# A node table seeded with its residual: x copied into the table in the first layer's down part, rows scaled before they are added

## What is computed

```
def _layer(x, node_idx, edge_idx, norm_n2e, norm_e2n, W_n2e, W_e2n):
    h = x @ W_n2e
    e = relu(segment_sum(norm_n2e * h[node_idx], edge_idx))
    n = segment_sum(norm_e2n * (e @ W_e2n)[edge_idx], node_idx)
x1 = relu(_layer(x, ..., W0_n2e, W0_e2n))
x2 = _layer(x1, ..., W1_n2e, W1_e2n)
x = layernorm(x + x2)
```

## Time and profile before

| what | value |
|---|---|
| time, median of 3 runs | 6743.85 us (6737.83 to 6748.29) |
| span of the profiled execution | 6891.4 us |
| share of the span busy: PE, DVE, ACT, POOL | 62%, 69%, 48%, 58% |
| DMA, mean over the span | 237 GB/s, 1634 MB in 646,111 packets |
| hardware queue (SP), software queue (POOL) | 1234.83 MB, 394.18 MB |

### The profile page before, as it was taken

How to read it: one execution, slowest core, us unless ns; L and a number is a source line. 1 busy time by engine, 2 the same in 40 slices (tenths; PEclk the granted TensorE clock), 3 DMA queues, 4 the chain that set the end, 5 groups by cost and what they waited for, 6 DMA issues and landing times. The chain is left out here.

```text
span 6891.4 us, 79060 instructions
## 1 busy us (share of the span) xinstructions
PE 4257.5 (62%) x18989; PEld 3141.2 (46%) x18989; DVE 4783.1 (69%) x15487; ACT 3305.7 (48%) x7376; POOL 4010.9 (58%) x3167
## 2 busy tenths in 40 slices
PE   2568883038885788499866677988885677600000
PEld 1247773037774666377612223547774566500000
DVE  6635544645454877599599996866665999587666
ACT  0023331013332555288656665758885788633333
POOL 4757776757775788767155426611113666277776
PEclk9779996569998999799978778989998899855555
DMA  7845445864544999799688988989996677477665
GB/s 278 287 121 79 76 75 147 335 197 75 79 76 89 328 350 351 219 326 342 200 293 304 312 273 318 379 290 328 331 336 222 231 258 247 175 261 242 236 227 193
DMA packets 646111, 1634.06 MB, mean 237 GB/s; under 512 B 128454, under 2 KB 283878, under 8 KB 630290
## 3 DMA queue, kind: packets, MB, share of 16 engines
q1 hardware_dynamic: 459954, 1234.83, 51.9%
q0 software_dynamic: 185696, 394.18, 21.4%
HBM read 816.50 MB, written 813.62 MB: 237 GB/s over the span
## 5 line engine op out<-in xcount | busy, mean ns | idle before, releaser
L822 POOL DMA_INDIRECT NS<-e_tot,e_idx x392 | 648.6, 1655 | 298.1 <-ACT e_tot L1080 222.4
L2304 ACT ACTIVATE l_z<-l_a,l_nb,l_rs 128x256 f32<-128x256 f32 x1176 | 612.7, 605 | 411.3 <-DMA out_dram<-l_z,k_ids 248.1
L1691 POOL DMA_INDIRECT l_eg<-HBT,k_nsrc x392 | 461.8, 1178 | 391.2 <-DVEq L1916 151.3
L956 DVE TENSOR_SCALAR e_eq<-e_pk,z_skey 128x128 f32<-128x128 f32 x588 | 204.2, 348 | 637.1 <-DMA NS<-e_tot,e_idx 608.1
L2181 POOL DMA_INDIRECT out_dram<-l_z,k_ids x392 | 432.0, 1102 | 150.9 <-issue 115.1
L1734 PE MATMUL l_pb<-l_jx,k_ones 128*128 128x128 f32 x26 | 4.3, 304 | 788.3 <-DVE l_jx L1971 788.3
L1080 ACT ACTIVATE e_tot<-e_pa 128x520 f32<-128x520 f32 x196 | 118.6, 605 | 759.7 <-DMA NS<-e_tot,e_idx 748.6
L2226 PE MATMUL l_pm<-k_w_L3b,l_zt 128*128 128x258 f32 x1568 | 404.5, 417 | 126.8 <-ACT l_o L2274 121.8
L2475 DVE BATCH_NORM_STATS2 l_bs<-l_a 128x6 f32<-128x256 f32 x1176 | 467.2, 420 | 10.5 <-issue 3.5
L1223 POOL DMA_INDIRECT XH<-n_o,z_home x392 | 398.0, 1015 | 118.1 <-issue 113.1
L2342 ACT ACTIVATE l_a<-l_a,l_eshare 128x64 f32<-128x64 f32 (+1 forms) x1372 | 382.0, 371 | 124.4 <-DVE l_eshare L1953 67.6
(11 more groups left out here) (409 smaller groups left out, 13538.8 us busy)
## 6 DMA issues: line engine op xcount, KB each, us to landing
NS<-z_zero SPq DMA_DIRECT2D x200, 520.0 KB
HBT<-l_o SPq DMA_DIRECT2D x196, 528.0 KB
l_a<-HBT SPq DMA_DIRECT2D x196, 528.0 KB
GSUMS<-l_erun SPq DMA_DIRECT2D x72, 1056.0 KB
l_a<-XH SPq DMA_DIRECT2D x98, 528.0 KB
HA<-n_o SPq DMA_DIRECT2D x98, 528.0 KB
l_a<-HA SPq DMA_DIRECT2D x98, 528.0 KB
n_r<-NS SPq DMA_DIRECT2D x98, 520.0 KB
```

The source lines that it names most:

```text
L822: pool.indirect_dma_start(out=nodes, out_offset=bass.IndirectOffsetOnAxis(ap=idx[q % DEEP][:, k:k + 1], axis=0), in_=tot[q % 2][:, k, :], ...
L1691: pool.indirect_dma_start(out=self.g[b % self.ng][:, k, :], out_offset=None, in_=self.table, in_offset=bass.IndirectOffsetOnAxis(ap=self.i ...
L2304: last = act.activation(z[:, j, 0:D], a[:, j, 0:D], ACT.Identity, bias=self.nb[b][:, col:col + 1], scale=self.rs[b][:, col:col + 1])
```

## The change

In layer e0's down part SP copies x into NS1, HBM to HBM, 512 rows a DMA in rows of 4 KB, two such copies behind each of the 49 loads of z, and clears the 256 spare rows and 128 rows past the last node. The 100 clears of NS1 in e1's up part are gone. `inv`, the scale of each edge's gathered row, is kept for all 49 tiles in e1; ACT's copy of a pair's total becomes two instructions of 256 columns with that scale, since the count of edges of a gathered node is also the count of the node that its edge goes back to. NS1 has rows of 256 columns, not 260, and already holds x when the sums are added. Node stage n0 loads NS1 alone into `a`, and has neither counts nor the addition; it has eight buffers each of `a` and `o`.

```diff
+def copy_rows(eng, table, x, n, sem):
+    if n == TAILN:
+        eng.dma_start(table[TAIL0:N, :]..., x[TAIL0:N, :]...).then_inc(sem, 16)
+    else:
+        eng.dma_start(table[n * BLK:(n + 1) * BLK, :].rearrange("(p j) w -> p (j w)", j=J),
+                      x[n * BLK:(n + 1) * BLK, :].rearrange("(p j) w -> p (j w)", j=J)).then_inc(sem, 16)
+def clear_spare_rows(eng, table, zero, sem):
+    spare = NPAD - 2 * P
+    eng.dma_start(table[spare:NPAD, :].rearrange("(p j) w -> p j w", j=2), zero[:, 0:2, 0:D]).then_inc(sem, 16)
+    eng.dma_start(table[N:N + P, :], zero[:, 0, 0:D]).then_inc(sem, 16)
...
+    filled = NREAL + 2 if scaled else CLEARS
-        inv = [s.sb(f"inv{b}", [P, J]) for b in range(2)]
+        inv = s.sb("inv", [P, TR, J]) if scaled else None
-        tot = [s.sb(f"tot{b}", [P, 2, SW]) for b in range(2)]
+        tot = [s.sb(f"tot{b}", [P, 2, ow]) for b in range(2)]
...
-                        pe.matmul(pa[:, 1, 0:SW], e[:, 1, :], mt[:, 1, :], start=True, stop=True).then_inc(s_tot, 1)
+                        pe.matmul(pa[:, 1, 0:ow], e[:, 1, :], mt[:, 1, 0:ow], start=True, stop=True).then_inc(s_tot, 1)
...
-                        act.activation(tot[q % 2][:], pa[:, :, 0:SW], ACT.Copy).then_inc(s_cp, 1)
+                        if scaled:
+                            for k in range(2):
+                                c = column(q) + k
+                                last = act.activation(tot[q % 2][:, k, :], pa[:, k, 0:ow], ACT.Copy, scale=inv[:, c // J, c % J:c % J + 1])
+                        else:
+                            last = act.activation(tot[q % 2][:], pa[:, :, 0:ow], ACT.Copy)
+                        last.then_inc(s_cp, 1)
...
                     sp.dma_start(z[n % RR][:], sumv[:, J * t:J * (t + 1), :]).then_inc(s_z[n % RR], 16)
+                    if seeds:
+                        seeded, sem, x = seeds
+                        if n == 0:
+                            clear_spare_rows(sp, seeded, S["zero"], sem)
+                        for c in range(NREAL * n // TR, NREAL * (n + 1) // TR):
+                            copy_rows(sp, seeded, x, c, sem)
...
-    RA, RR, RO = 7, 4, 7
+    RA, RO = 8, 8
...
-                            sp.dma_start(a[t % RA][:], A["x"][t * BLK:(t + 1) * BLK, :]...).then_inc(s_in[t % RA], 16)
-                        sp.dma_start(r[t % RR][:], T["NS1"][t * BLK:(t + 1) * BLK, :]...).then_inc(s_rin[t % RR], 16)
+                            sp.dma_start(a[t % RA][:], T["NS1"][t * BLK:(t + 1) * BLK, :]...).then_inc(s_in[t % RA], 16)
...
-        "NS1": nc.dram_tensor("NS1", (NPAD, SW), F32).ap(),
+        "NS1": nc.dram_tensor("NS1", (NPAD, D), F32).ap(),
...
-                                      up=(T["NS0"], S["cleared0"], EARLY, CLEARS), early=early,
+                                      up=(T["NS0"], S["cleared0"], EARLY, CLEARS), early=early, seeds=(T["NS1"], S["cleared1"], A["x"]),
-                                  up=(T["NS1"], S["cleared1"], 0, CLEARS), homes=(S, V, T), gather=T["HOME"])
+                                  up=(T["NS1"], S["cleared1"], 0, 0), homes=(S, V, T), gather=T["HOME"])
```

More of the change, by code:

```diff
@@ L681, in store, with hyper_layer_phase @@
                      self.T["HOME"].rearrange("(n p j) o -> p n (j o)", p=P, j=J)).then_inc(self.s_ho, 16)
-def hyper_layer_phase(nc, S, tag, table, tw, sums, w1, w2, nodes, clear, up, scatter=None, listing=None, homes=None, gather=None, early=None):
+def hyper_layer_phase(nc, S, tag, table, tw, sums, w1, w2, nodes, clear, up, scatter=None, listing=None, homes=None, gather=None, early=None, seeds=None):
     RR = 3
@@ L692, in hyper_layer_phase @@
     scaled = tw > D
+    ow = nodes.shape[1]
+    filled = NREAL + 2 if scaled else CLEARS
     with Scope(nc, tag) as s:
@@ L817, in _ @@
                         if q == 1:
-                            pool.wait_ge(clear, 16 * CLEARS)
+                            pool.wait_ge(clear, 16 * filled)
                         else:
@@ L1013, in _ @@
                         e, mt = eq[q % DEEP], m[q % DEEP]
-                        pe.matmul(pa[:, 0, 0:SW], e[:, 0, :], mt[:, 0, :], start=True, stop=False)
-                        pe.matmul(pa[:, 0, 0:SW], e[:, 2, :], mt[:, 1, :], start=False, stop=True)
-                        pe.matmul(pa[:, 1, 0:SW], e[:, 1, :], mt[:, 1, :], start=True, stop=True).then_inc(s_tot, 1)
+                        pe.matmul(pa[:, 0, 0:ow], e[:, 0, :], mt[:, 0, 0:ow], start=True, stop=False)
+                        pe.matmul(pa[:, 0, 0:ow], e[:, 2, :], mt[:, 1, 0:ow], start=False, stop=True)
+                        pe.matmul(pa[:, 1, 0:ow], e[:, 1, :], mt[:, 1, 0:ow], start=True, stop=True).then_inc(s_tot, 1)
                     if tick == EVICT:
@@ L1142, in first_nodes_phase @@
     TN = NREAL
-    LD, ADD, VAR, NORM, TURN, ZT, PROD, EVICT, STORE = 0, 2, 3, 5, 6, 7, 8, 9, 10
-    RA, RR, RO = 7, 4, 7
+    LD, STAT, VAR, NORM, TURN, ZT, PROD, EVICT, STORE = 0, 2, 3, 5, 6, 7, 8, 9, 10
+    RA, RO = 8, 8
     with Scope(nc, tag) as s:
         a = [s.sb(f"a{b}", [P, J, D]) for b in range(RA)]
-        r = [s.sb(f"r{b}", [P, J, SW]) for b in range(RR)]
         o = [s.sb(f"o{b}", [P, J, XW]) for b in range(RO)]
-        inv = [s.sb(f"inv{b}", [P, J]) for b in range(2)]
         bs = [s.sb(f"bs{b}", [P, 2 * J, 6]) for b in range(2)]
@@ L1170, in first_nodes_phase @@
         s_os = [s.pool_sem(S, f"out_scattered{b}") for b in range(RO)]
-        count_lk = Links(s.sem("count_steps"))
         stat_lk = Links(s.sem("row_stats_ready"))
@@ L1306, in variance, with stats @@
                     dve.tensor_scalar(ve[b][:], mv[b][:, :, 1], EPS, None, ALU.add).then_inc(s_var, 1)
[L1308 to L1313, removed]
-                    count_lk.link(dve.reciprocal(iv[:], iv[:]))
-                    yield
-                    count_lk.settle(dve)
+                def stats(t):
                     dve.wait_ge(s_in[t % RA], 16 * (t // RA + 1))
                     for j in range(J):
-                        last = dve.scalar_tensor_tensor(at[:, j, :], rt[:, j, 0:D], iv[:, j:j + 1], at[:, j, :], ALU.mult, ALU.add)
-                        if j < J - 1:
-                            yield
-                    last.then_inc(s_u, 1)
-                    yield
-                    dve.wait_ge(s_u, t + 1)
-                    for j in range(J):
-                        stat_lk.link(dve.bn_stats(bs[t // 2 % 2][:, t % 2 * J + j, :], at[:, j, :]))
+                        stat_lk.link(dve.bn_stats(bs[t // 2 % 2][:, t % 2 * J + j, :], a[t % RA][:, j, :]))
                         yield
@@ L1338, in _ @@
                         parts.append(variance(*q))
-                    if tile(tick, ADD) is not None:
-                        parts.append(add(tick - ADD))
+                    if tile(tick, STAT) is not None:
+                        parts.append(stats(tick - STAT))
                     take_turns(parts)
```

16 lines of the change are left out of this document (6 added, 10 removed).

## The result

The changed kernel took 6852.85 us, median of four runs (6839.86 to 6863.19), against 6743.44 us before on the same chip: 1.0154 times as long, 95% interval 1.0137 to 1.0172, +109 us. The sign was forecast; the forecast time, 6794 us, was 59 us too low, and the result lies 3 us above the range, 6690 to 6850 us.

What follows compares the result with a forecast made beforehand. It took the down parts as bound by chains of landing, two POOL issues and transfer, and n0 by POOL. Terms -32 - 30 - 10 + 122 = +50 us on 6743.85 gave 6794 us, range 6690 to 6850.

Steps and rivals of the forecast that it cites:

- Term 1: e1's up part: without the clears of NS1, shorter gathers, fewer DVE waits and an earlier end, -32 us (-20 to -40).
- Term 4: e0's down part: copies take turns with scatter-adds at 0.33 us a packet, +2.9 us in 42 pairs, +122 us.
- rival (a): e0's down part: copies run at one-sided pace, 0.163 us a packet, costing 57 us; net -15, 6729 us; chance 0.25.
- Term 2: Node stage n0 without counts, addition and second load: faster scatters and an earlier start, -30 us (-10 to -42).
- Term 3: e1's down part: shorter rows speed the scatter-adds and ACT's split copy costs nothing, -10 us.
- rival (d): e1's down part: ACT's copy on the chain, +25 us, or PE loses clock; 6819 us; chance 0.05.
- (b): e0's down part: copies hide in idle head and gap of each pair, costing 17 us; net -55, 6689 us; chance 0.19.
- (c): e0's down part: all copy work passes on and z comes late, 222 us; net +150, 6894 us; chance 0.08.

Runs made afterwards that it cites:

- e0: Not a run: a layer of the kernel, in whose down part the change places the copies; its adds take 672.4 us before, 807.2 after.
- e12_before: The kernel before, unedited, profiled on the chip where it runs in 6742 us; 6746.14 us, a single run.
- the first experiments: e1_before, e2_copy4k, e3_copy1k and e4_sbuf_fill, on a chip where the kernel before takes about 6890 us.
- e2_copy4k: Changed kernel with its copies cut into packets of 4 KB; 6989.16 us, 1.0143 of the kernel before on the same chip.
- e1_before: The kernel before, unedited, run again for a profile; 6890.52 us, ratio 0.9998.
- e3_copy1k: Changed kernel with its copies cut into rows of 1 KB; 6973.11 us, 1.0115 of the kernel before on the same chip.
- e4_sbuf_fill: Changed kernel writing zeros from SBUF in place of x, in packets of 4 KB; 6987.44 us, 1.013 of the kernel before.
- e13_after: The changed kernel, unedited, profiled on the same chip as e12_before; 6852.24 us, 1.0165 of the kernel before.
- e14_copy_e1up: Changed kernel with all 98 copies in e1's up part, in the clears' place, on the chip of e12_before; 6701.74 us, 0.9944 of the kernel before.
- e9_gate_two: Changed kernel with both copies held by a semaphore wait to the head of a pair without z; 6850.5 us, 0.9964 of the kernel before.
- e10_gate_one: Changed kernel with one copy at each of 42 heads of pairs without z, 14 before the first pair, 42 in e1's up part; 6839.71 us, 0.9948.

## Why the prediction was right, and where it was wrong

**Term 1, the clears (-32 us): the step that failed.** The step charged the clears with waits and a late end that they did not make, and took a gain of 32 us from leaving them out. Measured +5 us (290.8 to 295.7), which is no gain; the untouched stretches differ by nearly as much. The working took three numbers for the price of the clears: 13 us of gathers above 1.00 us, 8 us of waits for DVE, 12 us of a late end. The last two weren't the clears'. With clears, on a chip as fast as that of the timing (e12_before), the waits for DVE are 0.3 us in place of the earlier trace rows's 8.5, and between the last gather and the joining of the runs there are 7.6 us, not the 21 of the earlier trace rows:

```profile
1362.16 0.99 POOL L792 DMA_INDIRECT e_g<-NS,z_src  x1 [0.30 <-issue]
...
1369.79 0.50 PEld L1005 LDWEIGHTS e_po<-e_run,k_join 128*128 128x128 f32 x2 [268.34 <-DVEq L888]
```

What they were is in DVE's waits in this stretch (engine, tile, line, what it waited for: us, times, longest). The profile that the prediction read has

```profile
DVE e_run L885 <- issue: 30.9, 19, 4.2
...
DVE e_run L885 <- remote: 17.4, 10, 3.5
```

the kernel before again, on the chip of the first experiments,

```profile
DVE e_run L885 <- remote: 27.9, 15, 4.9
DVE e_run L885 <- issue: 21.3, 20, 2.7
DVE e_g L870 <- remote: 15.1, 10, 2.2
```

and on the chip of 6742 us, the same kernel and stretch:

```profile
DVE e_inv L863 <- DMA e_g<-NS,z_src: 85.1, 45, 6.3
```

On the chip of the first experiments, DVE stands between two steps of its own for 64 us, and no transfer ends those waits; on the last it hardly does (0.5 us). Taking the clears away there won 9 us in e2_copy4k (from the first gather to the joined rows 299.6 us, 308.9 in e1_before), 5 in e3_copy1k and 2 in e4_sbuf_fill. I had noted that the profile's span was 2.2% above the timing and carried a difference in us over from it; but most of this term was made of what sets the two chips apart. The 13 us of longer gathers were real in the row and not the clears' either: their mean is 1.049 us with clears and 1.071 without. What sets it is open.

**Term 4, the copies (+122 us): the size nearly right, by a wrong way.** Measured +134.8 us. In the two profiles of the changed kernel pairs with copies last 10.2 and 10.3 us and the others 6.8, as forecast; by 42 pairs the copies cost 3.2 us each (134.8/42) in place of 2.9. The packets were to take 0.33 us for 4 KB; they took 0.17, rival (a)'s pace, for which the working had 0.9 to 1.8 us a pair. They were to take turns with the adds' from 2.7 us on; in fact the second add had no turn until they were nearly through. And z was to be through at 2.7 us, in the idle head; in e13_after SP issued it 1.6 us into the pair (median; 0.0 in e12_before), and in 26 of the 42 pairs its last packets started only at 5.3 us, so that most of its work, 1.8 us, no longer hid. A price twice too high made up for the two delays left out: that the total came out near was luck, and only the cut packets, the zeros from SBUF and the moved copies tell this from the right reason. (The working's 0.153 us for an add packet does not follow from the 37.2% beside it, which gives 0.163; that would add some 5 us to the forecast.) The DMA share of e0's down part, 0.53 against 0.75 forecast, had already spoken against the price. The Trainium skill's page "DMA: Bandwidth & Descriptors" gives 207 to 214 GB/s each way for copies from HBM to HBM in "Latency and other measured facts", measured with rows 512 KB apart or padded by 4 KB; here the two copies at the head of the pair of e9_gate_two, 1.05 MB, took 4.1 us from their first packet to the end of their last, 253 GB/s each way, so that the measurement decides against it for this layout.

**Term 2, n0 (-30 us): right.** Measured -34.1 (25.6 + 8.5): the scatters' mean fell from 1.021 to 0.982 us, 15.5 us of 25.6, and issuing by 5.0. The groups in e12_before and e13_after:

```profile
L1223 POOL DMA_INDIRECT XH<-n_o,z_home x392 | 400.3, 1021 | 114.2 <-issue 111.4 <-ACT n_o L1269 1.6 <-DVE n_o L1285 1.2
```

```profile
L1245 POOL DMA_INDIRECT XH<-n_o,z_home x392 | 384.8, 982 | 114.0 <-issue 106.4 <-DVE n_o L1307 7.6
```

A tile takes 5.86 us (forecast 5.95). The first scatter came 30.8 us after the first load, in place of 40.4; 26 was forecast. Steady part and start were mis-sized against one another, the sum wasn't.

**Term 3, e1's pairs (-10 us): right.** -5.7 us, and -12.8 in e14_copy_e1up. ACT's second instruction is not on the chain: rival (d) would have made it 25 us longer.

**The rivals.** (b), copies that hide in the idle head, holds in a kernel whose copies wait for the head: e9_gate_two and e10_gate_one. The prediction said what spoke against it for this one, that the copies are issued when the head is over. That was most of the reason but not all of it: where z and the copies were issued at the head together, the pair still lasted 9.6 us. (c) had 222 us for the copies, 1.6 times what they cost. (a) had the pace right and the price too low.

**The arithmetic.** 134.8 - 122 is 13 us, the clears 37, n0 and e1 together 0, and 8 us lie before the first add (+3.9) and behind the last scatter of n0 (+4.4). The former isn't the fourteen early copies: e14_copy_e1up, which has none, reaches its first add at 413.4 us, 3 us later than the kernel before too. I can't say what they are. 13 + 37 + 8 = 58 of the 59 us missed. With the clears at nothing the sum would have been +82.

## What to carry to other kernels

Give a transfer a place in time, not only a stretch with room: an idle share of one half held 1 MB for 0.7 us at the head of a 7 us pair of dependent adds, and the same 1 MB issued some 3 us later, behind z, made it 10 us long; one semaphore wait was the difference. And before traffic is taken out of a full stretch, ask whether its bound, here POOL at 1.37 us a gather, waits for that traffic at all: full DMA engines with nobody waiting are the best place for it. When the profile is of a slower chip than the timing, a term made of waits that no transfer ends is not to be counted.

## What the runs showed of the hardware that I had not expected

- SP's queue joins the contiguous rows of a copy into packets of 32 KB, 16 to a 512 KB DMA, at 1.35 us each (mean; median 1.23), some 0.17 us for 4 KB. Cut into packets of 4 KB they take 0.159 us (median) whether both sides are HBM or the source is SBUF.
- A scatter-add with accumulation, issued while z and two copies of SP's queue are in the engines, starts about 3 us late (first packet 7.1 against 4.2 us into the pair, on the mean), and 2 us late with packets of 4 or 1 KB (6.3); pairs are nearly as long with packets of 4 or 1 KB as with 32 KB. The runs show the delay and that the place cures it; what in the chip makes it was not found.
- Chips differ by 2.2% on the same program, 6742 to 6892 us at clocks within 0.01, part of it in idle time between DVE's own instructions (64 us of it in e1's up part on one chip, 0.5 on another).
